# A graph-attention layer on one core: edges one unit ahead, the order of a unit's three VectorE steps, and products split around the next transposes

## The chip, the cores and the metric

The kernel runs on one core of a Trainium2 chip. The metric is the device time of one execution in microseconds (us), the median of several runs. Before the change it is 671.59 us (3 runs, 671.34 to 671.65). The engines of the core run side by side, each its own list of instructions in order, and wait for each other through semaphores: TensorE (PE) multiplies, ScalarE (ACT) and VectorE (DVE) work elementwise, GpSimd (POOL) and SyncE (SP) here mostly issue DMAs.

## The reference

```python
def reference(x, adj, W, a):            # x 8192x64 float32, adj 8192x8192 int32, W 64x64, a 128x1
    h = maximum(layernorm(x), 0)
    Wh = h @ W
    e = (Wh @ a[:64])[:, None] + (Wh @ a[64:])[None, :]
    e = leaky_relu(e, 0.2)
    att = softmax(where(adj > 0, e, -9e15), axis=1)
    return x + elu(att @ Wh)
```

Each entry of `adj` is 1 with probability 1/2048. The matrix alone is 268 MB that has to be read from memory once.

## The kernel before, in words

The exponential of a leaky ReLU of a sum splits into two cases, by the sign of the sum, and in each case into a factor of the row and a factor of the column. So the kernel makes no scores. For each entry it makes one byte that says: no edge, edge with a positive sum ("up"), edge with a negative sum ("down"). Those bytes, read as 8-bit floats, are the stationary matrices of products with the weighted columns `V` (float16, high and low parts). PE adds up two sums of 130 columns for each block of 128 rows, one over the ups and one over the downs, and a row factor joins them.

**The tiling.** Work goes in 128 *units*. A unit is 128 rows by 4096 columns of `adj`, so a block of 128 rows has two units. Eight units, which is four blocks of rows, are a *body*; there are 16 bodies (`NI`), and `i` is the body and `k` (0 to 7) the unit in it. Bodies 0 and 1 are written out by hand between the preparations. Bodies 2 to 15 run in loops with one pattern on each engine, the last one with a few branches of its own.

**A unit** goes through these steps:
- load: POOL issues a DMA of 1 MB (2 MB of int32 in memory, turned into bfloat16 on the way) into one of 8 slots of `adj_ring` (L448). The load of unit n waits until the edges of unit n-8 were made (`s_edge`).
- edges (E): DVE, L728 (`edges`), `code` = 0xC0 where there is an edge. `code` has 4 buffers.
- signs: ACT, L525 (`step`), into one of 2 buffers of `sign`, three units ahead.
- codes (C): DVE, L746 (`codes`), signs and edges into the final byte.
- transposes (T): PE, L1048, 16 of them into one of 2 pairs of PSUM banks (`transpose_unit`); they wait for the codes.
- copy: ACT, L533 (`copy_unit`), from PSUM to `codeT`; it waits for the transposes.
- ups (U): DVE, L752 (`find_ups`), from `codeT` to `ups` (2 buffers); it waits for the copy.
- products: PE, L1068 and L1070 (`multiply_unit`), 32 column blocks with 2 matmuls each; they wait for the ups.

**The order in a body before.** PE: transposes of k+1, then all products of k. ACT: copy of k+1, at k = 0 and 6 a small copy of sums (L538), signs of k+3, at k = 2 the negative part (L544, L546). DVE: codes of k+1, ups of k, at some k the steps on finished sums (below), then edges of k+4 (`FAR`, bodies 2 to 5) or of k+2 (`NEAR`, bodies 6 to 15). The steps on finished sums are `take_sums` (L766, L774; k = 1 and k = 7), `divide` (L781, L785, L787, L789; k = 1) and `result` (L795, L798; k = 4). SP stores a body's rows when `result` is done and loads the next body's `x`.

**The end.** The last tile is loaded in two halves, and `last_edges` (L738) makes their edges. `finish(b)` (L935 to L956) then does all last steps of one block; the last of them needs the exponential of ACT (`z_exp`).

`general_*` functions are another path for inputs for which the split would be too coarse; it is not taken here.

Of the kernel before, what the change touches and what calls it, by code (L numbers as in the profile page):

```python
# [31 lines left out]
def build_gat(nc, x, adj, W, a, out, s_nodes):  # L32
# [7 lines left out]
    HB = JB // 2  # L40
# [8 lines left out]
    BU = 2 * KE  # L49
    NI = JB // KE  # L50
# [9 lines left out]
    with ctx:  # L60
# [126 lines left out]
        s_up = sem("ups_written")  # L187
        s_mult = sem("unit_multiplied")
# [206 lines left out]
        with nc.Block() as block:  # L395
# [77 lines left out]
            def _(act):  # L473
# [187 lines left out]
                def body(i, last=False):  # L661
                    for k in range(BU):
                        if not (last and k + 1 >= BU):
                            copy_unit(i, k + 1)
                        if k == 0:
                            copy_lows(i * BU - 2, 1)
                        if k == 6 and not last:
                            copy_lows(i * BU + KE + 2, 0)
                        if k == 5 and last:
                            copy_lows_of(0)  # L670
                        if not (last and k + 3 >= BU):
                            step(i, k + 3)
                        if k == 2:
                            negative_part(i - 1)

                def copy_lows_of(b):
# [20 lines left out]
            def _(dve):  # L697
# [77 lines left out]
                                                       scalar=ab[:, B:B + 1] if isinstance(B, int) else ab[:, bass.ds(B, 1)],  # L775
                                                       in1=parts[:, o, k, 0], op0=ALU.mult, op1=ALU.add).then_inc(s_sum2, 1)

                def divide(i):

                    dve.wait_ge(s_sum2, (i + 1) * KE)  # L780
                    nc.vector.scalar_tensor_tensor(out=fill[:, :, :], in0=sums[:, :, F:FE].to_broadcast([P, KE, FE]),  # L781
                                                   scalar=0.0, in1=tot[:, :].unsqueeze(1).to_broadcast([P, KE, FE]),
                                                   op0=ALU.is_equal, op1=ALU.mult).then_inc(s_lone, 1)
                    dve.wait_ge(s_lone, i + 1)
                    nc.vector.tensor_tensor(sums[:, :, :], sums[:, :, :], fill[:, :, :], ALU.add).then_inc(s_fix, 1)  # L785
                    dve.wait_ge(s_fix, i + 1)
                    nc.vector.reciprocal(rden[:, :], sums[:, :, F]).then_inc(s_rden, 1)  # L787
                    dve.wait_ge(s_rden, i + 1)
                    nc.vector.tensor_tensor(hp, sums[:, :, 0:F],  # L789
                                            rden[:, :].unsqueeze(2).to_broadcast([P, KE, F]), ALU.mult).then_inc(s_hp, 1)  # L790
# [121 lines left out]
                take_sums(1, 1)  # L912
                codes(1, 7)
                find_ups(1, 5)
                divide(0)
                codes(2, 0)
                result(0)
# [9 lines left out]
                def finish(b):  # L927

                    def after(k):
                        dve.wait_ge(z_step, 7 * b + k)  # L930

                    B = (NI - 1) * KE + b
                    r = rden[:, b:b + 1]
                    dve.wait_ge(z_low, b + 1)
                    nc.vector.tensor_tensor(parts[:, b // 2, b % 2], lows[:, b // 2, b % 2],  # L935
                                            acc[b // 2][b % 2].rearrange("p (s l f) -> p s l f", s=2, l=2)[:, :, 0],
                                            ALU.add).then_inc(z_step, 1)
                    after(1)
                    nc.vector.scalar_tensor_tensor(out=sums[:, b], in0=parts[:, b // 2, b % 2, 1], scalar=ab[:, B:B + 1],
                                                   in1=parts[:, b // 2, b % 2, 0], op0=ALU.mult, op1=ALU.add).then_inc(z_step, 1)  # L940
                    after(2)
                    nc.vector.scalar_tensor_tensor(out=fill[:, b], in0=sums[:, b, F:FE].to_broadcast([P, FE]), scalar=0.0,
                                                   in1=tot[:, :], op0=ALU.is_equal, op1=ALU.mult).then_inc(z_step, 1)
                    after(3)
                    nc.vector.tensor_tensor(sums[:, b], sums[:, b], fill[:, b], ALU.add).then_inc(z_step, 1)
                    after(4)
                    nc.vector.reciprocal(r, sums[:, b, F:FE]).then_inc(z_step, 1)
                    after(5)
                    nc.vector.tensor_scalar(neg[:, b], sums[:, b, 0:F], r, 0.0, ALU.mult, ALU.min).then_inc(z_neg, 1)
                    nc.vector.tensor_scalar(hp[:, b], sums[:, b, 0:F], r, 0.0, ALU.mult, ALU.max).then_inc(z_step, 1)  # L950
                    after(6)
                    dve.wait_ge(s_xg, NI * 16)
                    nc.vector.tensor_tensor(hp[:, b], hp[:, b], xg[:, b], ALU.add).then_inc(z_step, 1)
                    after(7)
                    dve.wait_ge(z_exp, b + 1)
                    nc.vector.scalar_tensor_tensor(out=res[:, b], in0=neg[:, b], scalar=-1.0, in1=hp[:, b], op0=ALU.add,  # L956
                                                   op1=ALU.add).then_inc(z_res, 1)


                FAR, NEAR, CHANGE = 4, 2, 6  # L960

                def body(i, lead, start=0, last=False):
                    before = 0 if isinstance(i, int) and i == 2 else i - 1
                    for k in range(BU):
                        if not (last and k + 1 >= BU):
                            codes(i, k + 1)
                        find_ups(i, k)
                        if k == 1:
                            take_sums(before, 1)
                            divide(i - 1)  # L970
                        if k == 4:
                            result(i - 1)
                        if k == 7 and not last:
                            take_sums(i, 0)
                        if last and k == BU - 2:
                            finish(0)
                        if last and k + lead == BU - 1:
                            last_edges()
                        elif k >= start and not (last and k + lead >= BU):
                            edges(i, k + lead)  # L980

                body(2, FAR)
                with dve.Fori(3, CHANGE) as i:
                    body(i, FAR)
                body(CHANGE, NEAR, start=FAR - NEAR)
                with dve.Fori(CHANGE + 1, NI - 1) as i:
                    body(i, NEAR)
                body(NI - 1, NEAR, last=True)
                for b in range(1, KE):
                    finish(b)  # L990
                general_vector(dve)

            @block.tensor
            def _(pe):
# [53 lines left out]
                        last = nc.tensor.transpose(into[:, g * P:(g + 1) * P], mine[:, g * P:(g + 1) * P], identb[:, :])  # L1048
                    last.then_inc(s_T, 1)

                def multiply_unit(i, k, first=False):
                    body, b, h = place(i, k)
                    o = b // 2
                    sums_of = acc[o][b % 2]
                    early_half = isinstance(body, int) and body == 0
                    begins, stops = h == 0 or early_half, h == 1 or early_half
                    if begins and b % 2 == 0:
                        pe.wait_ge(s_acc[o], ONE + (i * 2 + k // KE + 1) // 2 if isinstance(i, int) and i < 2 else ONE + i + 1)
                    pe.wait_ge(s_up, i * BU + k + 1)
                    up8, down8 = [m.bitcast(F8).rearrange("p (g q b) -> p g b q", q=P, b=2)  # L1060
                                  for m in (ups[:, k % 2], codeT[:, k % RC])]
                    for j in range(HB):
                        jb = h * HB + j
                        if first and jb % RR == 0:
                            pe.wait_ge(s_lo, 2 * (jb // RR + 1))
                        if j == 0 or first and jb % RR == 0:
                            pe.sem_inc(s_go, 1)
                        nc.tensor.matmul(sums_of[:, 0:FP], up8[:, j // 2, j % 2], V[:, jb, 0:FP],  # L1068
                                         start=begins and j == 0, stop=False, skip_group_check=True)
                        last = nc.tensor.matmul(sums_of[:, FP:2 * FP], down8[:, j // 2, j % 2], V[:, jb, FP:2 * FP],  # L1070
                                                start=False, stop=stops and j == HB - 1, skip_group_check=True)
                    last.then_inc(s_mult, 1)

                transpose_round(0)
                pe.wait_ge(s_w, 32)
# [67 lines left out]

                def body(i, last=False):
                    for k in range(BU):
                        if not (last and k + 1 >= BU):
                            transpose_unit(i, k + 1)
                        multiply_unit(i, k)

                with pe.Fori(2, NI - 1) as i:  # L1150
                    body(i)
# [24 lines left out]
```

## Time and profile before

| | |
|---|---|
| median of 3 runs | 671.59 us (671.34 to 671.65) |
| the profiled execution's own time | 671.83 us |
| its span, first to last instruction | 670.0 us |
| mean granted clock of TensorE | 0.989 of full speed |
| PE / ACT / DVE / POOL busy | 95% / 94% / 92% / 12% of the span |
| the 16 DMA engines | busy in all slices but the last two |
| moved by DMA | 141.05 MB written; 272.70 MB read from memory |

A row of the timeline has the start in us from the span's start, the length in us, the engine, the line, the operation, what it writes and reads, and how often in a row; in brackets stands how long the engine was idle before it and what ended that. A row of the chain of waits has the start, the length and what the chain was in. Matmuls are pipelined: one lasts 0.22 us, the next one starts some 0.06 us after it. So do the instructions of ACT and DVE in part: what an instruction costs its engine is read from start to start.

### The profile page before, as it was taken

The page shows a single profiled execution, that of the slowest core. Times are in us where ns is not written, and L with a number is a line of the kernel's source. Part 1 is how long each engine was busy: PE and PEld are TensorE (multiplying, and loading weights), DVE is VectorE, ACT ScalarE, POOL GpSimd, SP SyncE. Part 2 cuts the span into 40 slices and gives each one's busy share as a digit, 9 for nine tenths or more (in the row PEclk, how much of TensorE's full clock was granted, in tenths as well). Part 3 has the DMA queues.
Part 4 walks back from the last instruction along what each step waited for, and adds up shares of the span by engine and source line. Part 5 has one row for each costly group of instructions (what it writes and reads, how often), then busy time and mean ns, then how long its engine had stood idle before and what let it go on. Part 6 is the DMA issues. An engine that isn't in the chain of part 4 may idle for free.

```text
span 670.0 us, 23442 instructions
## 1 busy us (share of the span) xinstructions
PE 635.0 (95%) x10422; PEld 622.4 (93%) x10422; DVE 619.5 (92%) x654; ACT 631.1 (94%) x372; POOL 82.7 (12%) x149
## 2 busy tenths in 40 slices
PE   4878999999999999999999999999899998989997
PEld 4758999999999999999999999999899998989997
DVE  5999999999999999889999999998989989898997
ACT  5799999899999999999999999999899998989982
POOL 7101201101111111000101101010110110101000
PEclk9988999999999999999999999999899999999999
DMA  9999999999999999999999999999999999999980
GB/s 211 217 214 217 215 216 217 217 217 217 218 215 217 217 216 216 218 215 217 216 217 217 216 216 215 218 216 216 217 218 217 215 216 218 215 217 217 216 182 21
DMA packets 32240, 141.05 MB, mean 211 GB/s; under 512 B 3664, under 2 KB 15696, under 8 KB 15952
## 3 DMA queue, kind: packets, MB, share of 16 engines
q0 software_dynamic: 18576, 134.23, 96.0%
q1 hardware_dynamic: 13168, 6.29, 4.2%
q8 instruction: 24, 0.39, 0.2%
q10 hardware_dynamic: 464, 0.07, 0.1%
q14 instruction: 8, 0.07, 0.0%
HBM read 272.70 MB, written 2.10 MB: 410 GB/s over the span
## 4 chain that ended last, share of the span: by engine, by line
ACT 32%; DMA 28%; PE 20%; DVE 11%; issue 7%; POOL 1%; ACTq 0%; DVEq 0%
DMA adj_ring<-in_adj 28%; ACT work L525 23%; ACT work L533 7%; DVE code L728 7%; PE psum L1070 6%; PE psum L1068 6%; PE psum L1048 3%; DVE code L746 1%; PE psum L1037 1%; PE psum L1015 1%; DVE work L752 1%; DMA work<-in_x 1%; PE psum L1005 1%; POOL work L455 1%; ACT last_steps L538 1%
## 5 line engine op out<-in xcount | busy, mean ns | idle before, releaser
L1068 PE MATMUL psum<-V,work 128*128 128x130 f16 x4096 | 492.8, 219 | 0.6 <-DVE work L752 0.5
L1070 PE MATMUL psum<-V,work 128*128 128x130 f16 x4096 | 493.1, 221 | 0.0
L525 ACT ACTIVATE work<-trow,Wh 128x4096 int8<-128x4096 f32 x128 | 477.6, 3735 | 0.0
L1068 PEld LDWEIGHTS psum<-V,work 128*128 128x128 fp8e4 x4096 | 402.2, 98 | 0.9 <-issue 0.9
L1070 PEld LDWEIGHTS psum<-V,work 128*128 128x128 fp8e4 x4096 | 397.8, 97 | 0.0
L728 DVE TENSOR_SCALAR code<-adj_ring 128x4096 uint8<-128x4096 bf16 x127 | 290.5, 2288 | 13.7 <-DMA adj_ring<-in_adj 13.7
L746 DVE SCALAR_TENSOR_TENSOR code<-work,code 128x1024 int32<-128x1024 int32 x128 | 156.6, 1223 | 13.3 <-ACT work L525 11.0
L1048 PE MATMUL psum<-identb,code 128*128 128x128 bf16 x2048 | 137.3, 221 | 17.1 <-DVE code L746 13.7
L533 ACT COPY work<-psum 128x1024 int32<-128x1024 int32 x128 | 130.7, 1024 | 16.0 <-PE psum L1048 15.6
L1048 PEld LDWEIGHTS psum<-identb,code 128*128 128x128 bf16 x2048 | 121.0, 99 | 22.0 <-DVE code L746 11.7
L448 POOL DMA_DIRECT2D adj_ring<-in_adj x127 | 72.3, 570 | 524.7 <-DVE code L728 517.0
L752 DVE TENSOR_SCALAR work<-work 128x1024 int32<-128x1024 int32 x128 | 87.8, 686 | 1.0 <-ACT work L533 0.9
L774 DVE SCALAR_TENSOR_TENSOR last_steps<-last_steps,ab 128x65 f32<-128x65 f32 x60 | 14.5, 284 | 3.9 <-DVE last_steps L766 2.0
L1005 PE MATMUL psum<-ident,work 128*128 128x128 f32 x32 | 6.9, 387 | 8.7 <-POOL work L455 8.7
L1005 PEld LDWEIGHTS psum<-ident,work 128*128 128x128 f32 x32 | 5.6, 202 | 9.2 <-issue 8.3
L538 ACT ACTIVATE last_steps<-psum 128x260 f32<-128x260 f32 x30 | 12.5, 415 | 0.9 <-PE psum L1070 0.9
L766 DVE TENSOR_TENSOR last_steps<-last_steps,psum 128x260 f32<-128x260 f32 x30 | 12.5, 418 | 0.0
L508 ACT ACTIVATE trow<-psum 128x1024 f32<-128x1024 f32 x8 | 8.4, 1092 | 2.5 <-PE psum L1028 2.5
L1037 PE MATMUL psum<-Wh,ones 128*128 128x512 f32 x16 | 9.3, 724 | 0.8 <-DVE Wh L719 0.8
L1015 PE MATMUL psum<-early_sums,V 128*128 128x134 f32 x64 | 9.2, 303 | 0.7 <-DVE Wh L719 0.7
L1015 PEld LDWEIGHTS psum<-early_sums,V 128*128 128x128 f32 x64 | 8.8, 214 | 1.2 <-issue 1.2
L705 DVE TENSOR_REDUCE last_steps<-work 128x16 f32<-128x1024 f32 x4 | 4.9, 1217 | 5.1 <-DMA work<-in_x 5.1
(91 smaller groups left out, 153.7 us busy)
## 6 DMA issues: line engine op xcount, KB each, us to landing
adj_ring<-in_adj POOLq DMA_DIRECT2D x127, 1024.0 KB, 31.8
work<-in_x SPq DMA_DIRECT2D x4, 512.0 KB, 6.2
last_steps<-in_x SPq DMA_DIRECT2D x16, 128.0 KB, 13.9
out_y<-last_steps SPq DMA_DIRECT2D x15, 128.0 KB, 13.9
adj_ring<-in_adj POOLq DMA_DIRECT2D x2, 512.0 KB, 36.0
out_y<-last_steps SPq DMA_DIRECT2D x4, 32.0 KB, 1.5
early_sums<-in_L_gnn_W ACTq DMA_DIRECT2D x4, 16.0 KB, 5.3
a_sb<-in_L_gnn_a ACTq DMA_DIRECT2D x1, 0.5 KB, 4.1
```

The lines of the kernel that those rows point to most:

```text
L448: pool.dma_start(adj_ring[:, k % RT, :], adj_v[b // 2, b % 2][i, :, h * UW:(h + 1) * UW])\
L525: nc.scalar.activation(sign[:, k % 2].bitcast(I8), trow[:, h * UW:(h + 1) * UW], ACT.Sign, bias=(Wh[:, B, 0:1] if isinstance(B, int) else ...
L533: nc.scalar.copy(codeT[:, k % RC].bitcast(I32), unitT[k % 2].bitcast(I32)).then_inc(s_codeT, 1)
L538: nc.scalar.activation(into[:, o], acc_pair[o].rearrange("p k (s l f) -> p k s l f", s=2, l=2)[:, :, :, 1], ACT.Copy, scale=1.0 / SPLIT).t ...
L728: nc.vector.tensor_scalar(code[:, k % RM, :], adj_ring[:, k % RT, :], 0.0, float(EDGE), ALU.is_gt, ALU.mult).then_inc(s_edge, 1)
L746: nc.vector.scalar_tensor_tensor(out=mine, in0=sign[:, k % 2].bitcast(I32), scalar=DOWN, in1=mine, op0=ALU.bitwise_xor, op1=ALU.bitwise_an ...
L752: nc.vector.tensor_scalar(ups[:, k % 2].bitcast(I32), codeT[:, k % RC].bitcast(I32), 1, DOWN, ALU.logical_shift_right, ALU.bitwise_and).th ...
L1005: last = nc.tensor.transpose(hT_ps[b % 2][:, c // 4, (c % 4) * P:(c % 4 + 1) * P], xh[:, r:r + 2, :].rearrange("p r f -> p (r f)"), ident[ ...
L1015: last = nc.tensor.matmul(Wh_ps[i][:, c // (HP // 2), (c % (HP // 2)) * 2 * FX: (c % (HP // 2) + 1) * 2 * FX], pair(b * PR + i * HP + c), ...
L1048: last = nc.tensor.transpose(into[:, g * P:(g + 1) * P], mine[:, g * P:(g + 1) * P], identb[:, :])
L1068: nc.tensor.matmul(sums_of[:, 0:FP], up8[:, j // 2, j % 2], V[:, jb, 0:FP], start=begins and j == 0, stop=False, skip_group_check=True)
L1070: last = nc.tensor.matmul(sums_of[:, FP:2 * FP], down8[:, j // 2, j % 2], V[:, jb, FP:2 * FP], start=False, stop=stops and j == HB - 1, sk ...
```

## The change

Bodies 0 and 1 keep their order. From body 2 on:
- DVE does, in each unit, edges of k+1, ups of k, codes of k+1. Before it was codes of k+1, ups of k, edges of k+4 or k+2. Since bodies 0 and 1 leave the edges four units ahead, body 2 makes none in its first three units (`ahead=3`).
- PE does the first half of the products of k, then the transposes of k+1, then the second half. The wait for the ups stands before the first half.
- `divide` is cut in two: `fill_lone` (L781, L785) at k = 2 and the division itself at k = 3; `result` goes from k = 4 to k = 5. On ACT the negative part goes from k = 2 to k = 4.
- In the last blocks the step that needs the exponential is a function of its own (`store_ready`), put behind the last ups for block 0.

```diff
@@ ScalarE, body @@
-                        if k == 2:
+                        if k == 4:
                             negative_part(i - 1)
@@ VectorE @@
-                def divide(i):
+                def fill_lone(i):
 
                     dve.wait_ge(s_sum2, (i + 1) * KE)
...
                     nc.vector.tensor_tensor(sums[:, :, :], sums[:, :, :], fill[:, :, :], ALU.add).then_inc(s_fix, 1)
+
+                def divide(i):
+
                     dve.wait_ge(s_fix, i + 1)
...
-                FAR, NEAR, CHANGE = 4, 2, 6
-
-                def body(i, lead, start=0, last=False):
+                def body(i, last=False, ahead=0):
                     before = 0 if isinstance(i, int) and i == 2 else i - 1
                     for k in range(BU):
-                        if not (last and k + 1 >= BU):
+                        if last and k == BU - 2:
+                            last_edges()
+                        elif k >= ahead and not (last and k == BU - 1):
+                            edges(i, k + 1)
+                        find_ups(i, k)
+                        if not (last and k == BU - 1):
                             codes(i, k + 1)
-                        find_ups(i, k)
                         if k == 1:
                             take_sums(before, 1)
+                        if k == 2:
+                            fill_lone(i - 1)
+                        if k == 3:
                             divide(i - 1)
-                        if k == 4:
+                        if k == 5:
                             result(i - 1)
                         if k == 7 and not last:
                             take_sums(i, 0)
                         if last and k == BU - 2:
                             finish(0)
-                        if last and k + lead == BU - 1:
-                            last_edges()
-                        elif k >= start and not (last and k + lead >= BU):
-                            edges(i, k + lead)
-
-                body(2, FAR)
-                with dve.Fori(3, CHANGE) as i:
-                    body(i, FAR)
-                body(CHANGE, NEAR, start=FAR - NEAR)
-                with dve.Fori(CHANGE + 1, NI - 1) as i:
-                    body(i, NEAR)
-                body(NI - 1, NEAR, last=True)
+                body(2, ahead=3)
+                with dve.Fori(3, NI - 1) as i:
+                    body(i)
+                body(NI - 1, last=True)
+                store_ready(0)
                 for b in range(1, KE):
                     finish(b)
+                    store_ready(b)
@@ TensorE @@
-                def multiply_unit(i, k, first=False):
+                def multiply_unit(i, k, first=False, part=range(HB)):
...
-                    pe.wait_ge(s_up, i * BU + k + 1)
+                    if 0 in part:
+                        pe.wait_ge(s_up, i * BU + k + 1)
...
-                    for j in range(HB):
+                    for j in part:
...
-                    last.then_inc(s_mult, 1)
+                    if HB - 1 in part:
+                        last.then_inc(s_mult, 1)
...
                 def body(i, last=False):
                     for k in range(BU):
+                        multiply_unit(i, k, part=range(HB // 2))
                         if not (last and k + 1 >= BU):
                             transpose_unit(i, k + 1)
-                        multiply_unit(i, k)
+                        multiply_unit(i, k, part=range(HB // 2, HB))
```

How the instructions stand on DVE, in the loop over the first bodies with this pattern: L728 is edges, L746 codes, L752 ups, L766 and L774 the taking of sums. Before, units k = 0 and 1:

```order
L746 SCALAR_TENSOR_TENSOR code<-work,code 128x1024
L750 REGISTER_ALU
L752 TENSOR_SCALAR work<-work 128x1024
L726 REGISTER_ALU
L727 ISA
L728 TENSOR_SCALAR code<-adj_ring 128x4096
L746 SCALAR_TENSOR_TENSOR code<-work,code 128x1024
L750 REGISTER_ALU
L752 TENSOR_SCALAR work<-work 128x1024
L765 ISA
L766 TENSOR_TENSOR last_steps<-last_steps,psum 128x260
```

And after, the same units:

```order
L728 TENSOR_SCALAR code<-adj_ring 128x4096
L750 REGISTER_ALU
L752 TENSOR_SCALAR work<-work 128x1024
L746 SCALAR_TENSOR_TENSOR code<-work,code 128x1024
L728 TENSOR_SCALAR code<-adj_ring 128x4096
L750 REGISTER_ALU
L752 TENSOR_SCALAR work<-work 128x1024
L746 SCALAR_TENSOR_TENSOR code<-work,code 128x1024
L765 ISA
L766 TENSOR_TENSOR last_steps<-last_steps,psum 128x260
```

The edges went to the head of a unit, and the ups now come ahead of the codes, so that an instruction on the ups stands between the edges of a unit and its codes.

On PE, in the loop, before (L1048 transposes, L1068 and L1070 products; in brackets the semaphores that are waited for):

```order
L1068 MATMUL psum<-V,work 128x130
L1070 MATMUL psum<-V,work 128x130
L1048 MATMUL psum<-identb,code 128x128 [waits codes_of_a_unit_written,transposed_unit_copied]
L1048 MATMUL psum<-identb,code 128x128 x15
L1068 MATMUL psum<-V,work 128x130 [waits ups_written]
L1070 MATMUL psum<-V,work 128x130
```

After, the transposes (now L1055; products L1076 and L1078):

```order
L1076 MATMUL psum<-V,work 128x130
L1078 MATMUL psum<-V,work 128x130
L1055 MATMUL psum<-identb,code 128x128 [waits codes_of_a_unit_written,transposed_unit_copied]
L1055 MATMUL psum<-identb,code 128x128 x15
L1076 MATMUL psum<-V,work 128x130
L1078 MATMUL psum<-V,work 128x130
```

After, the place where a unit's products begin, 32 matmuls behind the transposes:

```order
L1076 MATMUL psum<-V,work 128x130
L1078 MATMUL psum<-V,work 128x130
L1076 MATMUL psum<-V,work 128x130 [waits sums_of_pair_taken_1,ups_written]
L1078 MATMUL psum<-V,work 128x130
L1076 MATMUL psum<-V,work 128x130
```

Before, 64 matmuls stand between a unit's transposes and the products of that same unit. After, 32 do.

## Rows read from the trace of the kernel before

**Rows 1.** The page: busy time, DMA, and the chain that ended last.
```profile
PE 635.0 (95%) x10422; PEld 622.4 (93%) x10422; DVE 619.5 (92%) x654; ACT 631.1 (94%) x372; POOL 82.7 (12%) x149
...
DMA  9999999999999999999999999999999999999980
...
DMA adj_ring<-in_adj 28%; ACT work L525 23%; ACT work L533 7%; DVE code L728 7%; PE psum L1070 6%; PE psum L1068 6%; PE psum L1048 3%; DVE code L746 1%; PE psum L1037 1%; PE psum L1015 1%; DVE work L752 1%; DMA work<-in_x 1%; PE psum L1005 1%; POOL work L455 1%; ACT last_steps L538 1%
```

**Rows 2.** The chain in order of time (start, length, what), 497 to 540 us.
```profile
497.72 2.30 DVE code L728
...
537.67 2.30 DVE code L728
```

**Rows 3.** Instructions on adj_ring: the loads, whole run, then 130 to 185 us.
```profile
DMA to landing us min/median/max: 7.9/32.4/38.1
...
DMA to landing us min/median/max: 22.9/26.3/28.8
```

**Rows 4.** Timeline of ACT, body 2 and the start of body 3.
```profile
131.42 1.01 ACT L533 COPY work<-psum 128x1024 int32<-128x1024 int32 x1 [2.19 <-PE psum L1048]
...
136.21 1.01 ACT L533 COPY work<-psum 128x1024 int32<-128x1024 int32 x1
...
140.72 1.02 ACT L533 COPY work<-psum 128x1024 int32<-128x1024 int32 x1
...
146.00 0.99 ACT L533 COPY work<-psum 128x1024 int32<-128x1024 int32 x1
...
173.57 1.05 ACT L533 COPY work<-psum 128x1024 int32<-128x1024 int32 x1
```

**Rows 5.** PE: transposes of unit 1 of body 2 in the timeline.
```profile
130.33 1.05 PE L1048 MATMUL psum<-identb,code 128*128 128x128 bf16 x16
```

**Rows 6.** PE: two neighbouring groups of transposes in the chain.
```profile
378.02 0.89 PE psum L1048 x16
...
382.65 0.89 PE psum L1048 x16
```

**Rows 7.** Timeline: PE waits for ups (97 us), and for codes (401 us).
```profile
96.99 0.68 DVE L752 TENSOR_SCALAR work<-work 128x1024 int32<-128x1024 int32 x1
...
97.82 0.22 PE L1068 MATMUL psum<-V,work 128*128 128x130 f16 x1 [0.51 <-DVE work L752]
...
400.06 1.23 DVE L746 SCALAR_TENSOR_TENSOR code<-work,code 128x1024 int32<-128x1024 int32 x1
...
401.34 1.07 PE L1048 MATMUL psum<-identb,code 128*128 128x128 bf16 x16 [0.15 <-DVE code L746]
```

**Rows 8.** Timeline of DVE, ups after a wait, then ordinary units of body 2.
```profile
132.47 0.69 DVE L752 TENSOR_SCALAR work<-work 128x1024 int32<-128x1024 int32 x1 [0.29 <-ACT work L533]
...
139.93 2.29 DVE L728 TENSOR_SCALAR code<-adj_ring 128x4096 uint8<-128x4096 bf16 x1
142.13 1.22 DVE L746 SCALAR_TENSOR_TENSOR code<-work,code 128x1024 int32<-128x1024 int32 x1
143.27 0.69 DVE L752 TENSOR_SCALAR work<-work 128x1024 int32<-128x1024 int32 x1
143.87 2.29 DVE L728 TENSOR_SCALAR code<-adj_ring 128x4096 uint8<-128x4096 bf16 x1
```

**Rows 9.** Timeline of DVE, the steps on finished sums, body 3.
```profile
170.78 0.42 DVE L766 TENSOR_TENSOR last_steps<-last_steps,psum 128x260 f32<-128x260 f32 x1
...
171.90 0.43 DVE L781 SCALAR_TENSOR_TENSOR last_steps<-last_steps,tot 128x260 f32<-128x260 f32 x1
...
172.83 0.18 DVE L787 RECIPROCAL rden<-last_steps 128x4 f32<-128x4 f32 x1
...
173.38 2.29 DVE L728 TENSOR_SCALAR code<-adj_ring 128x4096 uint8<-128x4096 bf16 x1
```

**Rows 10.** The chain in order of time, the end.
```profile
652.05 1.05 PE psum L1048 x16
...
665.26 0.29 ACT last_steps L679
```

More of the change, by code:

```diff
@@ L914, in _ @@
                 find_ups(1, 5)
+                fill_lone(0)
                 divide(0)
@@ L953, in finish, with store_ready @@
                     nc.vector.tensor_tensor(hp[:, b], hp[:, b], xg[:, b], ALU.add).then_inc(z_step, 1)
-                    after(7)
+                def store_ready(b):
+                    dve.wait_ge(z_step, 7 * b + 7)
                     dve.wait_ge(z_exp, b + 1)
@@ L1056, in multiply_unit @@
                     begins, stops = h == 0 or early_half, h == 1 or early_half
-                    if begins and b % 2 == 0:
+                    if begins and b % 2 == 0 and 0 in part:
                         pe.wait_ge(s_acc[o], ONE + (i * 2 + k // KE + 1) // 2 if isinstance(i, int) and i < 2 else ONE + i + 1)
-                    pe.wait_ge(s_up, i * BU + k + 1)
+                    if 0 in part:
+                        pe.wait_ge(s_up, i * BU + k + 1)
                     up8, down8 = [m.bitcast(F8).rearrange("p (g q b) -> p g b q", q=P, b=2)
                                   for m in (ups[:, k % 2], codeT[:, k % RC])]
-                    for j in range(HB):
+                    for j in part:
                         jb = h * HB + j
```

## The prediction

> **What bounds the kernel now.** I read the page first. Its busy shares rank nothing: PE, ACT and DVE all stand above 92%, and the DMA engines are full in 38 of 40 slices [rows 1]. The chain has two large names, DMA on `adj_ring` and ACT on L525 [rows 1]. Put in order of time it shows two regimes.
>
> Late in the run the end of the chain is DMA waits with edges between them. From the edges that start at 497.72 to those at 537.67, eight units later, it is 39.95 us [rows 2]: one body at the pace of the loads.
>
> Early in the run ACT sets the pace. The copy of unit 1 starts at 136.21 in body 2 and at 173.57 in body 3, so a body takes 37.36 us [rows 4]. An ordinary step from copy to copy is 136.21 to 140.72, 4.51 us; the one with the negative part is 140.72 to 146.00, 5.28 us [rows 4]. PE is close behind: transposes to transposes is 4.63 us, of which 0.89 are the transposes [rows 6], so the products of a unit take 3.74, and eight units 37.04.
>
> So compute is 2.6 us a body faster than the loads, starts behind them and catches up, and then the loads set the end. After the last big wait of PE (652.05) comes a tail; the last product ends just before 665.26, where ACT takes its sums [rows 10]. The loads were never short of orders: one landed 7.9 us after its issue on an empty queue, and 22.9 at least around 150 us, the rest of it being queue [rows 3].
>
> The question is therefore not how much work the change takes off. It takes off none. It is how long a body of compute may become before the catching up fails. Body 2 of PE begins at 130.33, the transposes of unit 1 before [rows 5], the first half products of unit 0 after. If there are 14 bodies of length P from there, the last unit without transposes, the last product ends at 130.33 + 14 P - 4.80 + 3.74 (4.80 being the length of a unit, below). For the 665.2 of before P may be 38.3 us. Under that the loads decide and nothing changes; over it every 0.1 us of a body costs 1.4 us.
>
> **The change, part by part.**
>
> *Products split around the transposes.* The copy and the ups of a unit lie between its transposes and its products. Before, 64 matmuls of the unit ahead covered them, 3.74 us. Now only its second half does, half of 3.74, which is 1.87. The loop that closes, from one first half to the next:
> - the first half itself: 1.87;
> - start of the transposes to start of the copy: 130.33 to 131.42, where ACT was waiting for them: 1.09 [rows 4, 5];
> - start of the copy to start of the ups: 131.42 to 132.47, where DVE was waiting: 1.05 [rows 4, 8];
> - start of the ups to the first product: 96.99 to 97.82, where PE was waiting: 0.83 [rows 7]. The hand-over was sometimes shorter: from DVE's codes to the transposes it is 1.28 for an instruction of 1.23, so 0.05 beyond its end [rows 7]; with ups of 0.69 that gives 0.74.
>
> Together 4.84, at the least 4.75, against 4.63 of PE's own work. I take 4.80, between the two since the trace has each form once here. PE then idles 0.1 to 0.2 us in front of the products of every unit. That is small, but it can't be made up: ACT and DVE have time to spare, yet each has to wait for its turn in the loop.
>
> *Ups ahead of codes.* The codes start 0.60 behind the ups (143.27 to 143.87 is what ups cost DVE [rows 8]), and the transposes can follow 1.28 later: 1.88 after the start of the ups. The first half ends 0.83 + 1.87 = 2.70 after it. So the codes are hidden behind the first half, by 0.8 us; if that half were not there PE would wait for them.
>
> *DVE's turn.* Edges cost 2.20 (139.93 to 142.13), codes 1.14 (142.13 to 143.27), ups 0.60 [rows 8], together 3.94, under 4.80. There are 0.86 us free per unit, and the steps on sums have to fit. `take_sums` costs 1.12 with registers (170.78 to 171.90), `fill_lone` 0.93 (171.90 to 172.83), the division 0.55 (172.83 to 173.38) [rows 9]. They stand between the codes of k+1 and the edges of k+2, and the ups of k+1 come behind those. So k = 1 becomes 3.94 + 1.12 = 5.06, k = 2 becomes 4.87; k = 3 fits. `result` is two instructions of the kind of `fill_lone`, about 0.9, and fits to within 0.05 (I count nothing). The `take_sums` at k = 7 I count as fitting too, and for the high end as another 1.12, which is 5.06.
>
> *ACT's turn.* 4.51 a unit, under 4.80. The negative part moves from k = 2 to k = 4 but takes as long, 5.28 [rows 4]. Before, this was inside the 37.36; now PE and DVE wait for the copy behind it: 5.28 for that unit. The small copies at k = 0 and 6 I count as hidden by the 0.29 us that ACT has free; there 131.42 to 136.21, a unit with one, took 4.79 [rows 4].
>
> *The sum of a body:* five plain units, 24.00, and 5.06 + 4.87 + 5.28 = 15.21: P = 39.21 us. The last product ends at 130.33 + 14 x 39.21 - 4.80 + 3.74 = 678.2, against 665.2: 13.0 us later.
>
> *Edges one unit ahead.* Each load is ordered by the edges eight units back, so POOL's orders come later, in body 2 by the three units without edges, at most 3 x 4.80 = 14.4 us. The loads that took 22.9 us at the least from issue to landing in bodies 2 and 3 [rows 3] would take 8.5 or more, still above the 7.9 of an empty queue. So the queue does not run dry. Should it, the loads would have to lose more than the 13 us by which compute is now the later, before it shows.
>
> The Trainium skill (DMA: Bandwidth & Descriptors, section Anatomy of one DMA) puts a DMA from GpSimd at about 2.0 us plus bytes over 436 GB/s, an estimate of 6.8 us for these 2.1 MB. By it the margin would be 1.7 us and not 0.6, and the chance of a dry queue smaller still. The trace's 7.9 decides.
>
> *SP's queue.* `result` at k = 5 puts the store of 128 KB and the load of `x` one unit later. The next `result` is a body away, and in the last body the load of `x` is needed by the first `finish`, some 6 us later, when no load of `adj` is in its way. Nothing.
>
> *The end.* The last `finish` begins when the last product ends and keeps its length, so the 13.0 us go through whole. Splitting off `store_ready` takes a wait for ACT off DVE in front of the last ups, and PE has the second half of unit 6 to do meanwhile. Nothing.
>
> The Trainium skill (TensorE: Matmul & The Clock Gate, section Back-to-back issue gap) says that a stream of weight load and matmul pairs sustains about 81 ns a pair at 128 columns. Here 64 products take 3.74 us, 58 ns each, and 16 transposes 0.89, 56 ns [rows 6]. By the page's figure, as an estimate, the half products would be 2.6 us, the loop 5.5, and PE alone 6.5 us a unit, over 850 us in all, which the kernel before already contradicts. The trace goes ahead, and I give that outcome no chance.
>
> **Against its own time.** The profiled execution took 671.83, of which the span is 670.0; with 13.0 it would be 684.8. The median of before is 0.2 lower, so I predict 684.6.
>
> **The rivals.**
>
> *A: the loop does not close, and the loads go on setting the end.* For it speaks that 4.63 to 4.84 is a small step, read from single waits, and that some of the steps on sums may overlap more than I count. Against it: P under 38.3 would need plain units of 4.63 and also less than 15.2 for the other three, while 5.28 is read off ACT directly. The time would be that of before, 671.6 less 0.3 for the shorter tail: 671.3. Chance 0.11.
>
> *B, on the other side: the same, and the tail becomes shorter.* In the last body PE waited for the codes of unit 6 until 652.05, and then had the transposes of two units and three products to do. With half the products of unit 5 done in that wait, the end would be up to 1.87 us earlier, less 0.60 for the ups that now stand ahead of those codes; were those hidden, 669.7. It decides only where the loads arrive last, so from P = 38.2 down. That product is also held by ups of unit 6, which come behind the last edges. Chance 0.05.
>
> *C: worse.* The loop takes in something more: a unit in which DVE's steps and ACT's negative part add up rather than standing in different units, or a clock that falls with the many small waits. Another 0.3 us a unit would be 34 us, some 718 us. What speaks against it: the three long units are k = 1, 2 and 4, and in between the loop has 0.3 us of slack on ACT and 0.86 on DVE. Chance 0.04.
>
> **How the numbers follow.** The forecast has 0.80. Its own range: plain units of 4.75 take 5 x 0.05 x 14 = 3.5 us off, 681.1; those of 4.84 add 2.8, and the second `take_sums` at 5.06 adds 0.26 x 14 = 3.6, together 691.0. As both highs are unlikely to come together, and as bits of 0.05 may hide here and there, I take 679 to 690 for it. The range for the record has to reach to A, as B, C and the edges of my own case already make up nearly 2 in 10: 671 to 690. What this kernel's measurement can tell from no change is about 0.2%, 1.3 us. Slower by more than that: forecast and C, 0.84. Within it: A, 0.11. Faster: B, 0.05.
>
> **What would show it.** In the profile after, PE should wait for the ups (L752) in front of nearly every unit, 0.1 to 0.2 us, and some 0.3 to 0.5 at k = 2, 3 and 5; a body from transposes to transposes should be 39.0 to 39.4 us from body 3 to body 15 alike; ACT should wait for the transposes in every unit; DVE's waits for the loads should be gone; the loads should take 9 to 15 us to landing at first and more later; and the last loads should land well ahead of their edges. Bodies that begin at under 38.3 us and end at 40 would be rival A. If PE hardly waits for the ups, my loop is wrong; if it waits, but for the codes, the order ups before codes is what costs.

## The result and the profile after

The changed kernel takes 731.1 us (median of 4 runs, 730.79 to 732.97), the kernel before 671.62 (4 runs, 671.34 to 671.75). The ratio is 1.0893, with a 95% interval of 1.088 to 1.0906. Forecast were 684.6 us and a range up to 690. The direction was right. Of the 59.5 us that came, the forecast had 13.

The page of the changed kernel (busy time, granted clock of TensorE in 40 slices, traffic):

```profile
span 729.5 us, 23456 instructions
...
PE 657.1 (90%) x10422; PEld 633.6 (87%) x10422; DVE 615.1 (84%) x654; ACT 638.3 (87%) x372; POOL 86.6 (12%) x149
...
GB/s 214 216 216 216 215 217 217 217 215 218 215 202 199 210 186 205 193 203 200 213 210 191 210 197 208 201 196 206 202 211 206 209 178 194 216 200 211 71 2 26
```

It answers to [rows 1]. PE is busy 22 us longer with the same number of instructions, and all engines stand idle more. In slices 12 to 37 DMA moves 178 to 216 GB/s, some 200 in the mean, where the page of before has 215 to 218 in most slices: compute now sets when a load is ordered. The waits, from the same kernel (who waited for whom, us in total, times, the longest):

```profile
ACT work L533 <- PE psum L1055: 71.3, 70, 5.9
PEld psum L1076 <- issue: 65.0, 107, 2.9
DVE work L752 <- ACT work L533: 56.4, 58, 5.5
PE psum L1076 <- DVE work L752: 43.9, 26, 2.7
DVE last_steps L798 <- ACT last_steps L546: 36.5, 14, 2.6
```

No wait of DVE for a load is left. The first four are at the places of the forecast's loop: copy for transposes, ups for copy, products for ups (the second is PE's weight loads, standing idle at the products). But PE's 43.9 us are not the loop's own small waits. 14 of the 26 are 2.64 us long, 36.9 us together, and the other 12, 0.4 to 0.9 us each, are nearly all at the first unit of a body. In front of the products of plain units PE is idle for only 0.05 to 0.1 us, as the last matmul is still running, and the list leaves that out; the loop has to be read from start to start. The fifth wasn't in the forecast: 14 times, once a body, `result` (now L798) waits 2.6 us for the exponential.

The loop, in the chain of waits of the changed kernel (start, length; the transposes of four units), against 378.02 and 382.65 in [rows 6]:

```profile
303.58 0.89 PE psum L1055 x16
308.43 0.89 PE psum L1055 x16
...
318.16 0.89 PE psum L1055 x16
323.01 0.91 PE psum L1055 x16
```

An ordinary unit is 4.85 us, where 4.63 had been. Now the timeline around the fifth wait, in body 4 (ACT, DVE and PE):

```profile
237.06 1.01 ACT L533 COPY work<-psum 128x1024 int32<-128x1024 int32 x1 [0.23 <-PE psum L1055]
237.97 3.71 ACT L525 ACTIVATE work<-trow,Wh 128x4096 int8<-128x4096 f32 x1
238.10 0.69 DVE L752 TENSOR_SCALAR work<-work 128x1024 int32<-128x1024 int32 x1 [0.82 <-ACT work L533]
238.71 1.22 DVE L746 SCALAR_TENSOR_TENSOR code<-work,code 128x1024 int32<-128x1024 int32 x1
240.81 1.05 PE L1055 MATMUL psum<-identb,code 128*128 128x128 bf16 x16
242.01 0.42 ACT L546 ACTIVATE last_steps<-last_steps 128x256 f32<-128x256 f32 x1
242.53 0.43 DVE L798 SCALAR_TENSOR_TENSOR last_steps<-last_steps 128x256 f32<-128x256 f32 x1 [2.60 <-ACT last_steps L546]
243.34 2.29 DVE L728 TENSOR_SCALAR code<-adj_ring 128x4096 uint8<-128x4096 bf16 x1
245.54 0.69 DVE L752 TENSOR_SCALAR work<-work 128x1024 int32<-128x1024 int32 x1
246.37 0.22 PE L1076 MATMUL psum<-V,work 128*128 128x130 f16 x1 [2.64 <-DVE work L752]
249.55 1.32 PE L1055 MATMUL psum<-identb,code 128*128 128x128 bf16 x16
```

The copy of unit 5 starts at 237.06. DVE takes the ups and the codes and is done with unit 5 at about 239.9. Next in its list stands `result`, and that needs the exponential, which ACT makes behind the copy and 3.6 us of signs, at 242.01. DVE stands still for 2.6 us. Behind `result` stand the edges of unit 7 and the ups of unit 6, and PE, with its first half of unit 6 ready to go, waits 2.64 us for those ups. The rows hold a last surprise: the half product that starts at 246.37 ends at 249.55, 3.18 us and not 1.87. The windows say why (length, busy us of PE, PEld, DVE, ACT, POOL, granted clock, DMA share, GB/s):

```profile
236.00:246.00 10.00, 7.68 (x131) 7.35 (x128) 6.54 (x7) 9.74 (x7) 0.61 (x2) 1.00 1.03 212
246.00:251.00 5.00, 4.63 (x53) 4.66 (x54) 3.56 (x3) 1.03 (x2) 0.97 (x2) 0.66 0.99 192
330.00:335.00 5.00, 2.37 (x41) 2.22 (x39) 5.00 (x5) 3.82 (x2) 0.53 (x1) 1.00 0.98 200
```

After the wait the granted clock was 0.66 over 5 us: part of them at 1.2 GHz, not 2.4. Two bodies later the same wait (2.63 us, up to 333.25) was followed by none of that. So there are two kinds of body: 41.9 us without a fall of the clock and mostly 43.2 to 43.6 with one. Eight of the 14 had one, by the units behind that wait, which were 1.3 to 1.6 us longer there.

### The profile page after: what moved, and what is told of

It is laid out like the page before. It is cut to its first block, busy times and chain, and to the rows that moved or that the text cites. A ratio compares the mean times of both kernels' runs of the same rounds, so it can differ in the third digit from the quotient of the medians.

```text
span 729.5 us, 23456 instructions
## 1 busy us (share of the span) xinstructions
PE 657.1 (90%) x10422; PEld 633.6 (87%) x10422; DVE 615.1 (84%) x654; ACT 638.3 (87%) x372; POOL 86.6 (12%) x149
## 4 chain that ended last, share of the span: by engine, by line
PE 60%; ACT 13%; DVE 12%; issue 12%; DVEq 1%; DMA 1%; POOL 1%; ACTq 0%
PE psum L1076 24%; PE psum L1078 22%; PE psum L1055 13%; ACT work L525 8%; ACT work L533 4%; DVE work L752 3%; DVE code L746 3%; DVE code L728 2%; DVE V L808 1%; PE psum L1022 1%; DVE last_steps L798 1%; ACT last_steps L546 1%; ACT last_steps L544 1%; DMA work<-in_x 1%; POOL work L455 1%
## 5 line engine op out<-in xcount | busy, mean ns | idle before, releaser
L1076 PE MATMUL psum<-V,work 128*128 128x130 f16 x4096 | 511.5, 221 | 49.0 <-DVE work L752 43.9
L1078 PE MATMUL psum<-V,work 128*128 128x130 f16 x4096 | 512.2, 223 | 0.0
L1076 PEld LDWEIGHTS psum<-V,work 128*128 128x128 fp8e4 x4096 | 405.2, 99 | 65.1 <-issue 65.0
L1078 PEld LDWEIGHTS psum<-V,work 128*128 128x128 fp8e4 x4096 | 401.8, 98 | 0.0
L728 DVE TENSOR_SCALAR code<-adj_ring 128x4096 uint8<-128x4096 bf16 x127 | 290.4, 2288 | 3.8 <-issue 3.8
L746 DVE SCALAR_TENSOR_TENSOR code<-work,code 128x1024 int32<-128x1024 int32 x128 | 155.8, 1217 | 0.0
L1055 PE MATMUL psum<-identb,code 128*128 128x128 bf16 x2048 | 141.2, 225 | 5.1 <-ACT trow L508 2.7
L448 POOL DMA_DIRECT2D adj_ring<-in_adj x127 | 76.2, 600 | 576.0 <-DVE code L728 565.4
L752 DVE TENSOR_SCALAR work<-work 128x1024 int32<-128x1024 int32 x128 | 88.2, 690 | 56.4 <-ACT work L533 56.4
L1055 PEld LDWEIGHTS psum<-identb,code 128*128 128x128 bf16 x2048 | 126.0, 101 | 6.1 <-ACT trow L508 3.0
L798 DVE SCALAR_TENSOR_TENSOR last_steps<-last_steps 128x256 f32<-128x256 f32 x15 | 6.4, 425 | 36.5 <-ACT last_steps L546 36.5
L774 DVE SCALAR_TENSOR_TENSOR last_steps<-last_steps,ab 128x65 f32<-128x65 f32 x60 | 14.9, 285 | 4.4 <-DVE last_steps L766 2.2
L766 DVE TENSOR_TENSOR last_steps<-last_steps,psum 128x260 f32<-128x260 f32 x30 | 12.5, 417 | 0.0
L1035 PEld LDWEIGHTS psum<-ident,Wh 128*128 128x128 f32 x64 | 7.1, 137 | 2.7 <-issue 2.7
L1035 PE MATMUL psum<-ident,Wh 128*128 128x128 f32 x64 | 7.8, 273 | 1.4 <-ACT trow L508 1.4
```

Of the source, the lines that this page charges most:

```text
L448: pool.dma_start(adj_ring[:, k % RT, :], adj_v[b // 2, b % 2][i, :, h * UW:(h + 1) * UW])\
L728: nc.vector.tensor_scalar(code[:, k % RM, :], adj_ring[:, k % RT, :], 0.0, float(EDGE), ALU.is_gt, ALU.mult).then_inc(s_edge, 1)
L746: nc.vector.scalar_tensor_tensor(out=mine, in0=sign[:, k % 2].bitcast(I32), scalar=DOWN, in1=mine, op0=ALU.bitwise_xor, op1=ALU.bitwise_an ...
L752: nc.vector.tensor_scalar(ups[:, k % 2].bitcast(I32), codeT[:, k % RC].bitcast(I32), 1, DOWN, ALU.logical_shift_right, ALU.bitwise_and).th ...
L774: nc.vector.scalar_tensor_tensor(out=sums[:, o * 2 + k], in0=parts[:, o, k, 1], scalar=ab[:, B:B + 1] if isinstance(B, int) else ab[:, bas ...
L798: nc.vector.scalar_tensor_tensor(out=hp, in0=hp, scalar=0.0, in1=xg[:, :, :], op0=ALU.max, op1=ALU.add).then_inc(s_pos, 1)
```

## The experiments

Each was run beside the kernel before, on the same chip. Two theories stood at the start. Theory 1: two separate losses, the loop through the split products and the wait of `result` in DVE's list, with the clock on top of the second. Theory 2: the new order on DVE, or the edges only one unit ahead (late orders to the load queue), make every unit long.

**The negative part one unit earlier**, in the changed kernel:

```diff
-                        if k == 4:
+                        if k == 3:
                             negative_part(i - 1)
```

> The changed kernel with the negative part of ScalarE one unit earlier, at k = 3 and not k = 4; all else as changed. Theory 1 (two separate losses: the split closes a loop of 4.85 us a unit, and the division's result at k = 5 makes VectorE wait 2.6 us for the exponential, behind which the edges and the ups of the next unit stand, after which TensorE's clock also falls): the wait of L798 goes, the unit of 7.4 to 8.7 us becomes 4.85, the one with the negative part 5.3; a body is 39.8 us instead of 41.9 to 43.8, the clock is back at 0.99, the time is about 691 us. Theory 2 (the order on VectorE or late orders to the load queue make every unit long; the wait for the exponential is a symptom): the time stays above 720 us.

690.49 us (ratio 1.029, 1.0273 to 1.0308), so 40.6 us less than the changed kernel for one number. The wait of L798 is gone from the list, the mean clock is 0.993 (changed kernel: 0.973), and bodies 5 to 14 take 39.75 us each. In its chain of waits plain units remain 4.85, and the one behind `take_sums` at k = 1 is 4.89:

```profile
329.52 0.89 PE psum L1055 x16
334.37 0.89 PE psum L1055 x16
339.26 0.89 PE psum L1055 x16
344.11 0.91 PE psum L1055 x16
```

That is theory 1 to within 0.5 us for the time. It also is the forecast's own model put to the test without the fault in it: 39.75 against the 39.21 of its sum.

**The products in one piece again**, VectorE and ScalarE as changed:

```diff
-                        multiply_unit(i, k, part=range(HB // 2))
                         if not (last and k + 1 >= BU):
                             transpose_unit(i, k + 1)
-                        multiply_unit(i, k, part=range(HB // 2, HB))
+                        multiply_unit(i, k)
```

> The changed kernel with TensorE's order of before (transposes of k+1, then all products of k); VectorE's and ScalarE's order as changed. Theory 1: plain units go back to 4.63 us, TensorE waits for the ups only in the unit behind the wait for the exponential, where 2.0 us are lost because the codes of unit 7 come late; a body is about 39.4 us, the time about 688 us. Theory 2: units stay at 4.85 us or more, over 715 us. A third, that the split is harmless: no change from 731 us.

698.45 us (ratio 1.0391, 1.0353 to 1.0429). Better than the 731.1 by 33 us, and 10 us worse than expected. The plain units are back at 4.63. The unit behind the wait is 6.8, so 2.2 us are lost where 2.0 were expected, but I had left the clock out; in the profiled execution it falls in bodies 2 to 12 and again in the last, and costs the unit after it 1.6 us more each time. That execution was the slowest of the four (703.75 us, mean clock 0.963; the fastest 695.79 at 0.975). Without the falls, 12 x 1.6 us, it would be some 684.5, as an estimate, and 688 was expected. Its timeline of PE, and a window:

```profile
240.65 1.60 PE L1055 MATMUL psum<-identb,code 128*128 128x128 bf16 x16 [2.02 <-DVE code L746]
246.88 1.05 PE L1055 MATMUL psum<-identb,code 128*128 128x128 bf16 x16
```

```profile
240.00:245.00 5.00, 4.35 (x48) 4.35 (x49) 4.47 (x4) 2.89 (x4) 0.53 (x1) 0.66 1.05 220
```

Now PE waits for the codes, not the ups, since in this order they stand behind the ups: the same stop of DVE reaches PE through another semaphore.

**Both together**: products in one piece, negative part at k = 3. Left of the change are the edges one unit ahead, the ups ahead of the codes and the spread.

> Both of the last two edits in the changed kernel: TensorE's order of before, and the negative part at k = 3. What is left of the change is edges one unit ahead, ups before codes, and the spread steps. Theory 1: bodies of 37.4 us again, the loads set the end, 671.6 us within 1.5. Theory 2 (order on VectorE, edges only one unit ahead): over 680 us.

672.04 us (ratio 1.0012, 1.0002 to 1.0021). The bodies take 37.6 us up to body 10 (38.1 in body 3) and 40.0 from body 11 on, and the waits for the loads are back:

```profile
DVE code L728 <- DMA adj_ring<-in_adj: 16.6, 25, 1.3
```

The order on DVE and the later orders to the load queue cost about 0.2 us a body (37.6 for 37.4), which the loads cover. Theory 2 falls.

**The split alone, in the kernel before** (its `multiply_unit` and PE's body replaced by those of the change):

> The kernel before with only TensorE's products split into halves around the transposes; VectorE and ScalarE as before. Theory 1: the loop of first half, transposes, copy, ups closes here too: plain units 4.85 us, and the unit with all steps on sums at k = 1 (2.6 us on VectorE between the ups of one unit and the edges, codes and ups of the next) 6.5 us; a body of about 41 us, the time 700 to 712 us. The rival, that the split is harmless without the new order on VectorE: 671.6 us.

710.95 us (ratio 1.0592, 1.0574 to 1.061). The chain of waits shows a plain unit and then the one behind all the steps on sums:

```profile
335.40 0.89 PE psum L1048 x16
340.25 0.89 PE psum L1048 x16
346.88 0.91 PE psum L1048 x16
```

4.85 and 6.63: the loop is the same with DVE's old order. And the steps at k = 1, which the whole products of before had covered but for 0.3 us (4.95 for 4.63 in most of the early bodies), now reach PE. A body is 41.2 us here, and 39.75 in the kernel above that has them spread and the new order on DVE; what the spread alone gives behind a split was not run.

**The spread alone, in the kernel before**: `fill_lone` at k = 2, division at k = 3, negative part at k = 4, `result` at k = 5.

> The kernel before with only the spread steps of the change: fill at k = 2, division at k = 3, negative part at k = 4, result at k = 5; orders of edges, ups, codes and products as before. Theory 1: the wait of the result for the exponential (2.5 us and more, behind it edges and codes) costs here too, 1.5 us a body and about as much again where the clock falls: a body of 39 to 40.4 us, 680 to 700 us. The rival, that the spread is harmless and only the split costs: 671.6 us.

678.73 us (ratio 1.0102, 1.0087 to 1.0118), a little under the expected range. The timeline of DVE:

```profile
228.90 0.68 DVE L752 TENSOR_SCALAR work<-work 128x1024 int32<-128x1024 int32 x1
232.52 0.42 DVE L798 SCALAR_TENSOR_TENSOR last_steps<-last_steps 128x256 f32<-128x256 f32 x1 [2.94 <-ACT last_steps L546]
...
233.32 2.28 DVE L728 TENSOR_SCALAR code<-adj_ring 128x4096 uint8<-128x4096 bf16 x1
```

`result` waits here too, 2.5 us in the mean and up to 3.6, and the whole products of a unit cover part of it. PE loses 1.6 to 1.7 us in a unit that is mostly 6.2 to 6.3, and a body is 38.7 to 38.8 us. The clock stays (mean 0.992); the range had allowed for falls. The wait is thus harmful by itself; behind the split the same unit loses 2.6 us (7.43 for 4.85).

**How much goes ahead of the transposes.** In the kernel with the negative part at k = 3, `HB // 2` in PE's body was replaced: by `HB // 4` (16 matmuls ahead), by `3 * HB // 4` (48) and by `3 * HB // 8` (24).

> The changed kernel with the negative part at k = 3 and only the first quarter of a unit's products (16 matmuls) ahead of the transposes, not the half. Theory 1: the loop is 0.94 + 2.98 = 3.9 us, under TensorE's own 4.63, so it no longer counts; bodies of 37.4 to 37.7 us, then the pace of the loads, 671.0 to 672 us, at best 0.5 us under the kernel before from the tail. A rival, that any wait for ups ahead of the transposes costs a hand-over of 0.2 us per unit: 4.85 us a unit and 690 us as with the half.

> The same with three quarters (48 matmuls) ahead of the transposes. Theory 1: loop 2.80 + 2.98 = 5.8 us in every unit, and as that is longer than VectorE's 5.4 and ScalarE's 5.3, these no longer show; all units 5.8, a body 46.3, the time about 784 us. The rival: 690 us.

> The changed kernel with the negative part at k = 3 and three eighths of a unit's products (24 matmuls) ahead of the transposes. Theory 1: loop 1.40 + 2.98 = 4.4 us, still under TensorE's 4.63, so bodies of 37.6 us and then the pace of the loads; at the end TensorE waits 0.2 us less in front of the transposes of units 6 and 7 than with a quarter: 670.2 to 670.6 us. If the loop counts before it is longer than 4.63 (several small delays adding up), the bodies are over 38 us and the time 671 us or more.

Three quarters: 781.22 us (2 runs; ratio 1.1637), where 784 was expected. Every unit of every body is 5.8 us, also those with the sums and the negative part:

```profile
311.39 0.91 PE psum L1055 x16
317.18 0.91 PE psum L1055 x16
322.95 0.89 PE psum L1055 x16
```

One quarter: 670.55 us (ratio 0.9988, 0.9979 to 0.9997), bodies of 37.6 us and then the loads' pace. Three eighths: 670.45 us (ratio 0.9984, 0.9975 to 0.9993). The time is as expected, the bodies are not: 38.2 us for the 37.6 expected, just under the 38.3 from which compute would set the end, and DVE's waits for loads are down to 4.8 us. So in a plain unit the loop is the share of products ahead (0.94, 1.40, 1.87, 2.80 us) plus 2.98 us for copy, ups and hand-overs, and it counts from 4.63 on: 4.63, 4.63, 4.85 and 5.78 us were measured. The 2.98 is read from the half (4.85 less 1.87), and the three quarters bear it out. In units with an added step it counts sooner: with three eighths the longest three are 4.79, 5.01 and 5.11 us, against 4.63, 4.65 and 5.01 with a quarter.

The last two are faster than the kernel before by 0.9 and 1.1 us, which their intervals only just tell from no change. The chain at the end shows where. First with a quarter, then with three eighths (the last row is the one behind the last product, at 665.26 in [rows 10]):

```profile
651.88 1.05 PE psum L1055 x16
656.68 1.05 PE psum L1055 x16
...
664.32 0.29 ACT last_steps L679
```

```profile
652.22 0.89 PE psum L1055 x16
657.02 0.89 PE psum L1055 x16
...
664.02 0.29 ACT last_steps L679
```

PE does part of the products while it waits for the codes of units 6 and 7, and is through 0.9 and 1.2 us earlier. All of it is at the end, as the loads set the rest.

## Why the prediction was right and wrong

- *Two regimes, and the question how long a body may become: right.* Everything under 38.3 us a body (while the loads don't yet set the pace) measured 670 to 672 us, everything over it was slower: 38.8 gave 678.7, 39.75 gave 690.5, 41.2 gave 711.0, 46.2 gave 781.2. Between 39.75 and 41.2 that is 20.5 us for 1.45 us a body, the 14 of the forecast. (The copies at 136.21 and 173.57 that the forecast reads as those of unit 1 are those of unit 2; the body's length is the same by either.)
- *The loop: right.* Forecast 4.75 to 4.84, taken 4.80, measured 4.85 (0.01 over the upper end, which had the hand-over of 0.83 read from one wait), in the changed kernel and with the split alone.
- *The step that failed: "`result` is two instructions of the kind of `fill_lone`, about 0.9, and fits to within 0.05 (I count nothing)".* I put the duration of the moved step into the sum and not what it waits for. The next paragraph of the forecast moves the negative part to k = 4 of ACT and notes that it ends 5.28 us after the start of the copy of unit 5. `result` needs just that, and DVE comes to it 2.9 us after the same start, behind ups of unit 5 and codes of unit 6. Before, the exponential was made at k = 2 and used at k = 4. The change makes it at k = 4 and uses it at k = 5, and since ACT's k = 4 begins with the copy that DVE's k = 5 waits for, the two run at the same time. The unit concerned took 7.43 us where the clock did not fall, against 5.28 in the sum: 2.15 us a body, 30 us in all. Moving the exponential one unit earlier gave 40.6 us back, the clock's share included.
- *Rival C: its first form was near the truth, and had too small a chance.* It named a unit in which DVE's steps and ACT's negative part add up, shared a chance of 0.04 with the clock, and was set aside because the long units are k = 1, 2 and 4. `result` is at k = 5 and was not among them, as it was counted at nothing.
- *The clock: named in rival C too, for the wrong reason.* Not the many small waits but the one long one was followed by falls, in 8 of 14 bodies of the profiled execution, 1.4 us each, 11.5 us in all. With the long wait gone the small ones stayed (13.8 us in 27 of them in the list of waits) and the clock was 0.993.
- *`take_sums` at k = 7: "I count as fitting too".* It did not. With 0.34 us in which DVE was at the loop's branch it made that unit 5.37 us, 0.57 over the 4.80 counted and more than my high end of 5.06. At k = 1 the unit was 4.89 for the 5.06 counted. Together 0.4 us a body.
- *Codes hidden behind the first half, no cost for one unit of lead and for the queue: right.* With the products in one piece and the wait gone the kernel takes 672.0 us, and in the changed kernel PE waits for the ups, not for the codes. The queue did come near to empty in the changed kernel (7.2 to 11.3 us to landing between 200 and 600 us, median 9.8, where the shortest in the kernel before was 7.9), because compute no longer asked for more, and it did not matter: no edge waited for a load.
- *The tail: the 0.60 taken off did not show.* Rival B had up to 1.87 us for the half, less 0.60 for the ups. With a quarter or three eighths ahead, 0.94 and 1.40 us of products, there were 0.9 and 1.2 us, in kernels paced by the loads. With the half no loads set the end, and its tail stayed untested.
- *The start: a slip of 1.9 us, the other way.* The forecast starts its 14 bodies at 130.33 with the first half products of unit 0, behind the transposes of unit 1. The changed list has that half ahead of those transposes. In the changed kernel it begins at 128.40 and the transposes at 130.27:

```profile
128.40 0.22 PE L1076 MATMUL psum<-V,work 128*128 128x130 f16 x1
130.27 1.05 PE L1055 MATMUL psum<-identb,code 128*128 128x128 bf16 x16
```

In sum, of the 59.5 us: 13.0 as forecast, 30.1 for the wait of `result`, 11.5 for the clock, 2.8 for the loop's upper end (0.05 x 4 x 14, the unit with `take_sums` at k = 7 being counted apart) and 5.0 for `take_sums` (13 x 0.57 less 14 x 0.17). Off that go 0.9, as the first units of body 3 and of the last body were 4.85 and 4.97, not 5.37, and the 1.9 of the start. That makes 59.6.

The split is worth something only while loop, copy and ups fit into a unit's own work; as an estimate, 28 of a unit's 64 matmuls, at 58 ns each, would bring the loop to 4.63, and the half that the change chose is 32. Even 28 would most likely be too many, by the run with 24, whose bodies are 38.2 us of the 38.3 allowed. What isn't settled is why the clock fell after some waits of 2.6 us and not after others of the same length.

## What to carry to other kernels

When a step moves in an in-order list, don't ask only whether its duration fits but when its inputs are made, on the other engine, in that engine's own time; then name what is queued behind it. When work of an engine is put ahead of a wait, write down the loop that closes through the other engines: the part put ahead plus all hand-overs has to stay under the engine's own work per unit, and the right amount is read off that sum. Leave room for the units with an added step: three eighths, 0.25 us under by the sum, still made a body 0.6 us longer than a quarter.

## What the runs showed of the hardware that I had not expected

TensorE's granted clock was 0.66 over the 5 us after an idle stretch of 2.64 us, and equally after one of 2.02 us in the kernel with whole products. There bodies 2 to 12 each had one, and bodies 13 and 14, with the same wait of 2.02 us, had none. In the changed kernel it stayed at 1.00 after another wait of 2.63 us. The length of the wait alone doesn't decide. The kernel before had one such fall too, behind a wait of 1.86 us for the codes (body 11, where the loads set the pace), and none behind three later waits of 1.85, 1.86 and 1.73 us:

```profile
477.99 1.83 PE L1048 MATMUL psum<-identb,code 128*128 128x128 bf16 x16 [1.86 <-DVE code L746]
478.00:483.00 5.00, 5.00 (x60) 5.00 (x61) 4.78 (x5) 3.15 (x2) 0.53 (x1) 0.66 1.03 215
```

In the kernel with only the split, PE waited 2.02 us in body 2 and the clock stayed at 1.00:

```profile
140.74 0.22 PE L1069 MATMUL psum<-V,work 128*128 128x130 f16 x1 [2.02 <-issue]
140.00:145.00 5.00, 4.26 (x74) 4.29 (x75) 4.23 (x5) 2.81 (x3) 0.53 (x1) 1.00 1.05 221
```

Its 12 later waits, 1.7 to 1.8 us each, weren't followed by a fall either. Nor were the 14 waits for the codes, 1.4 to 1.8 us, in the kernel with only the spread steps. In the changed kernel a fall cost 1.3 to 1.6 us, on top of the wait that came before it.
